# Reordering a four-bit feed-forward by pairs of tiles, and a rotary attention with a third score buffer, in an eight-layer kernel

## The chip, the cores and the metric

The kernel is one program on one core of a Trainium2 chip. The metric is the device time of one execution in microseconds (us), and lower is better. Before the change three runs took 2469.4, 2476.17 and 2476.51 us, a median of 2476.17 us.

## The reference

The program computes two hybrid blocks one after the other on `x` of 8 sequences x 512 tokens x 128 channels. Only two kinds of layer matter here. The rest (a state-space scan, a linear attention, a forgetting attention, small normalised feed-forwards) is not touched.

The four-bit feed-forward occurs twice. Its input is normalised over the channels, rounded to a four-bit grid in blocks of 16, multiplied by four-bit weights, gated, and rounded again:

```python
def fp4_quant_dequant(x):                       # blocks of 16 along the last axis
    scale = jnp.maximum(jnp.max(jnp.abs(xb), axis=-1, keepdims=True) / 6.0, 1e-12)
    q = _GRID[jnp.searchsorted(_MID, jnp.abs(xb / scale))] * jnp.sign(xb / scale) * scale
def fp4_linear(x, w):
    return jnp.einsum('bsk,nk->bsn', fp4_quant_dequant(x), fp4_quant_dequant(w))
gate = fp4_linear(x, w_gate); y = fp4_linear(x, w_up)      # 128 -> 352
h = jax.nn.silu(gate) * y
out = fp4_linear(h, w_down)                                # 352 -> 128
```

The rotary attention occurs once, with 16 heads of 8 channels. Queries and keys are rotated, scores are `q k / sqrt(8)` over the 512 tokens of a sequence, then softmax, values, output projection and residual.

## The kernel before, in words

Every layer is one or more stages. A stage owns its buffers and semaphores and ends in a barrier of all engines. Inside a stage each engine has its own instruction list, written out by hand, and the lists meet only through semaphores. Each engine works strictly in the order of its list.

**The first feed-forward stage, `fx`,** quantises the input in four pairs of sequences, each pair one PSUM tile of 128 x 1024 values. TensorE centres the columns. ScalarE squares and sums them (`moments`). VectorE takes block maxima (`maxima`, L736), refines the root (`roots`), makes the scales (`codes`, L756 to L765, of which `above` is L758 and `both` L762) and multiplies them in (`xn`, L765). ScalarE then takes the scaled magnitude (`size`, L715). Rounding is done by adding and subtracting a large number, `mag = max(size, ROUND)`. VectorE computes `tot = max(size, ROUND) + xn` in one instruction (L770). GpSimd computes `mag` (L786), `q = tot - mag` (L790) and `xq = q * above` (L793). TensorE turns `xq` back and ScalarE stores it.

**The second feed-forward stage, `fh`,** walks over 32 tiles j of 128 tokens, four tiles (`NT`) to a sequence m. Per tile:

- TensorE: `gate(j+1)` (L823), `up(j)` (L827), and for the tile three steps older `end` (L835): three transposes of `hq`, and after each fourth tile the down projection (L842), six matmuls of 512 columns.
- ScalarE: `th = tanh(gate/2)` (L860), `size` of the previous tile (L866), and the two copies `ht` of the transposed tile (L872, L873).
- VectorE: `gt = (th + 1) * gate` (L880), the product with `up` (L883), `tot` of the previous tile (L888), the block maxima (L893), `above` (L896), its reciprocal (L898), and `xn` (L900). After every fourth tile it adds the down projection to the residual X (L912, and L914 for the last).
- GpSimd: `mag` (L921), `q` (L925), `hq` (L928).

There are two gate buffers, three up buffers and two transpose buffers in PSUM.

**The attention stage, `rt`,** walks over 8 sequences in a hardware loop, software-pipelined by `pipeline`. One sequence has 16 steps k. A step has two units of scores (L1912), each two matmuls that fill one of two score buffers of two PSUM banks. ScalarE takes the exponential of each unit (L1975, 128 x 1024 values, 256 in all). TensorE multiplies step k-1 by the values (`values`, L1923, eight matmuls with a ones column for the sum), into one of two output buffers. After every fourth step VectorE copies the output to SBUF (`osb`, L1986). TensorE turns it (`turn`, L1931), VectorE divides. Once per sequence follow `turn_back` (L1938), a copy `otc` on VectorE (L1999), `project` (L1943) and the residual (L2004). GpSimd lays out the values of each sequence (`va`, L1900). SyncE loads the query and key stacks half a sequence ahead.

## Time and profile before

| | |
|---|---|
| median of three runs | 2476.17 us |
| the profiled execution, its own time | 2476.36 us |
| its span | 2474.6 us |
| TensorE / VectorE / ScalarE / GpSimd busy | 79% / 67% / 56% / 41% |
| quantising stage `fx`, twice | 429.6 to 475.2 us, and again from about 729 us |
| feed-forward stage `fh`, twice | 476.1 to 621.6 us, and again from about 776 us |
| attention stage `rt`, once | 2158.6 to 2439.4 us |

Busy shares are averages over some thirty stages with different limits, so they say little about these three. In a row of the timeline the first number is the start, the second the length. A length covers the instruction from its start to its last write, and two instructions of one engine without a wait between them overlap by about 0.09 us. The distance between starts is therefore the better measure. A matmul in this number format is two instructions. "[0.64 <-PE ...]" is idle time before the instruction and what ended it.

### The profile page before, as it was taken

What the parts mean: (1) busy time and instruction counts of PE and PEld (TensorE: products, weight loads), DVE (VectorE), ACT (ScalarE), POOL (GpSimd) and SP (SyncE); (2) the same over time, 40 slices, a digit from 0 to 9 for tenths busy, and PEclk for the clock granted to TensorE, in tenths of its full rate; (3) what the DMA queues carried; (4) which work ended last, traced back from release to release, by engine and by line L of the source; (5) the groups of instructions that cost most, each with busy time, mean ns of one, the idle gap of its engine ahead of it and who ended that gap; (6) DMA issues with size and microseconds to landing.
All of it is one profiled execution on the core that took longest, in us unless ns stands there. A gap on an engine that the chain in (4) does not pass through costs nothing. (4 is left out here: it accounts for less than half of the span.)

```text
span 2474.6 us, 37339 instructions
## 1 busy us (share of the span) xinstructions
PE 1943.5 (79%) x11731; PEld 880.3 (36%) x11731; DVE 1648.7 (67%) x2449; ACT 1395.7 (56%) x2254; POOL 1013.6 (41%) x818
## 2 busy tenths in 40 slices
PE   5458885476784674799999999999998867588887
PEld 2123332333463331344444444444444423222222
DVE  5979995687436866778888888888886436611112
ACT  3446661422343323577777777777775533398884
POOL 0256661666016650245455555555545423700001
PEclk9779996688896877899999999999999978799999
DMA  2000000000000001111111111111111100411110
GB/s 87 0 13 0 0 0 0 0 1 1 0 0 0 1 1 50 37 38 58 57 60 56 59 61 60 56 56 56 60 60 57 44 18 26 102 40 50 44 45 34
DMA packets 66132, 85.94 MB, mean 35 GB/s; under 512 B 13345, under 2 KB 37217, under 8 KB 65889
## 3 DMA queue, kind: packets, MB, share of 16 engines
q1 hardware_dynamic: 60944, 81.37, 10.6%
q10 hardware_dynamic: 5040, 2.72, 0.4%
q8 instruction: 79, 1.29, 0.2%
q14 instruction: 69, 0.56, 0.1%
HBM read 72.12 MB, written 11.93 MB: 34 GB/s over the span
## 5 line engine op out<-in xcount | busy, mean ns | idle before, releaser
L1975 ACT ACTIVATE rt_p<-rt_ps_s 128x1024 f32<-128x1024 f32 x256 | 242.7, 1026 | 43.8 <-PE rt_ps_s L1912 43.1
L1618 DVE SCALAR_TENSOR_TENSOR fu_kv<-fu_ps_kv,fa_vec,fu_kv 128x511 f32<-128x511 f32 x366 | 252.6, 739 | 7.3 <-ACT fu_kv L1526 6.4
L1690 POOL TENSOR_TENSOR fu_p<-fu_p 128x768 f32<-128x768 f32 x64 | 116.9, 1826 | 260.3 <-PE fu_ps_n L1376 256.0
L1346 PE MATMUL fu_ps_s<-fu_qn,fu_kn 64*128 64x512 f32 (+3 forms) x1024 | 190.0, 468 | 7.3 <-ACT fu_p L1513 5.6
L601 POOL TENSOR_TENSOR scan_hC<-scan_h,scan_c 128x1024 f32<-128x1024 f32 x64 | 150.8, 2356 | 82.7 <-DVE scan_h L581 82.7
L1376 PE MATMUL fu_ps_n<-fu_p,fu_vt 128*64 128x512 f32 (+3 forms) x1024 | 166.0, 445 | 0.0
L526 PE MATMUL scan_ps_y<-scan_hC,w_ident 128*128 128x512 f32 x256 | 130.3, 632 | 40.9 <-POOL scan_hC L601 24.3
L1701 POOL TENSOR_TENSOR fu_num<-fu_num,fu_sg 128x512 f32<-128x512 f32 x64 | 81.4, 1272 | 172.1 <-DVE fu_sg L1651 172.1
L581 DVE TENSOR_TENSOR_SCAN scan_h<-scan_dA,scan_ps_b 128x1024 f32<-128x1024 f32 x64 | 146.4, 2287 | 2.2
L1923 PE MATMUL rt_ps_o<-rt_p,rt_va 128*32 128x512 f32 x1024 | 138.1, 612 | 4.6 <-POOL rt_va L1900 3.5
L1404 PE MATMUL fu_ps_kv<-w_XN,fa_wp 128*128 128x512 f32 x244 | 125.1, 636 | 18.1 <-DVE fu_cr L1583 15.4
L1346 PEld LDWEIGHTS fu_ps_s<-fu_qn,fu_kn 64*128 64x128 f32 x1024 | 82.6, 185 | 126.4 <-ACT fu_p L1530 52.1
L1912 PE MATMUL rt_ps_s<-ra_stackq,ra_stackk 48*128 48x512 bf16 x512 | 92.7, 390 | 41.4 <-ACT rt_p L1975 22.6
L1591 DVE SCALAR_TENSOR_TENSOR fu_og<-fu_num,fu_ow,fu_ro 128x512 f32<-128x512 f32 x64 | 81.1, 1267 | 58.0 <-POOL fu_num L1701 49.9
L1685 POOL TENSOR_TENSOR fu_kn<-fu_ks,fu_rb 128x512 f32<-128x512 f32 x64 | 99.1, 1549 | 40.6 <-DMA fu_rb<-rms_rows 40.5
L866 ACT ACTIVATE fh_size<-fh_ps_u 128x352 f32<-128x352 f32 x64 | 29.7, 464 | 151.9 <-DVE fh_ps_u L900 151.9
L1526 ACT ACTIVATE fu_kv<-fu_ps_kv,fa_vec 128x512 f32<-128x512 f32 x122 | 82.1, 687 | 51.4 <-PE fu_ps_kv L1404 47.2
L562 ACT ACTIVATE scan_c<-scan_ps_c 128x1024 f32<-128x1024 f32 x64 | 65.5, 1024 | 75.2 <-POOL scan_hC L601 46.4
L823 PE MATMUL fh_ps_g<-w_gate,ffn_xq 128*128 128x352 f32 x128 | 61.9, 573 | 56.8 <-DVE fh_gt L880 53.7
L1595 DVE TENSOR_REDUCE fu_nm<-fu_ps_m 128x2 f32<-128x1024 f32 x64 | 78.0, 1219 | 42.0 <-PE fu_ps_m L1369 42.0
L1900 POOL COPY rt_va<-ra_v 128x128 f32 x32 | 8.1, 296 | 232.8 <-PE rt_ps_o L1923 232.4
L1651 DVE SCALAR_TENSOR_TENSOR fu_sg<-fu_sg,fu_ps_s 128x512 f32<-128x512 f32 x64 | 44.0, 687 | 81.1 <-ACT fu_sg L1502 80.5
(350 smaller groups left out, 5178.6 us busy)
## 6 DMA issues: line engine op xcount, KB each, us to landing
fu_rb<-rms_rows SPq DMA_DIRECT2D x256, 128.0 KB, 2.9
fu_ro<-rms_rows SPq DMA_DIRECT2D x128, 128.0 KB, 2.9
ra_stackq<-rope_parts SPq DMA_DIRECT2D x168, 32.0 KB
ra_stackk<-rope_parts SPq DMA_DIRECT2D x168, 32.0 KB
rope_parts<-rp_q SPq DMA_DIRECT2D x24, 128.0 KB, 2.0
rope_parts<-rp_k SPq DMA_DIRECT2D x24, 128.0 KB, 2.0
rms_rows<-fu_r SPq DMA_DIRECT2D x14, 192.0 KB, 2.1
w_X<-in_xT SPq DMA_DIRECT2D x4, 512.0 KB
```

The costliest lines, as they stand in the source:

```text
L526: i = pe.matmul(yps[:, :], w.ident[:, :], hC[p % (BEHIND + 2)][:, j, :], start=(p == 0 and j == 0), stop=(p == PAIRS - 1 and j == 1))
L581: dve.tensor_tensor_scan(flat[0], flat[1], flat[2], 0.0, ALU.mult, ALU.add).then_inc(s.scan, 1)
L601: pool.tensor_tensor(hC[p % (BEHIND + 2)][:, :, :], hst[p % 2][:, :, :], csb[p % 2][:, :, :], ALU.mult).then_inc(s.hC, 1)
L1346: pe.matmul(sps[:, h, at:at + T - t * P], k[head(h), t * P:(t + 1) * P], q[head(h), t * P:T], start=(at == 0), stop=False)
L1376: m = pe.matmul(nps[head(h), t * P:T], VT[b % VR][:, t, head(h)], p[:, h, :], start=(t == 0), stop=(t == 2))
L1404: pe.matmul(projected(a, j), wp[:, g, 1 + j, :], XN[:, n, :], start=True, stop=True).then_inc(s.kvp, 1)
L1618: dve.scalar_tensor_tensor(acc, projected(a, k)[:, 0:T - j], vec[:, a % GA, at:at + 1], acc, ALU.mult, ALU.add).then_inc(done, 1)
L1685: pool.tensor_tensor(KN[u % 3][:, :], K[u % KR][:, :], RB[:, 1, :], ALU.mult).then_inc(s.kn, 1)
L1690: pool.tensor_tensor(tail, tail, P13[:, :, 0:3 * P], ALU.add).then_inc(s.d1, 1)
L1912: m = pe.matmul(sps[i][:, e, :], stack[1][rows, 2 * q4 + i, t * P:(t + 1) * P], stack[0][rows, 2 * q4 + i, :], start=True, stop=True)
L1923: m = pe.matmul(ops[q4 % 2][32 * j:32 * j + 32, :], va[:, t, 4 * q4 + j, :], pr[k % 2][j // 2][:, j % 2, :], start=(t == 0), stop=(t == NT ...
L1975: act.activation(pr[k % 2][i][:, :, :], sps[i][:, :, :], ACT.Exp, scale=DH_B ** -0.5).then_inc(s.exp, 1)
```

## The change

Three stages change. In `fx` and `fh` the instruction `mag` moves from GpSimd to VectorE, and `tot` becomes a plain addition of `mag` and `xn`. In `fh`:

- ScalarE applies silu itself. The VectorE instruction L880 is gone, and `w.down` is no longer halved in preparation.
- VectorE works on pairs of tiles. `above`, the reciprocal and `mag` each cover two tiles in one instruction.
- TensorE issues gate and up two tiles ahead, and there are four up buffers in place of three but one transpose buffer in place of two. The transposes run four tiles behind, and the down projection of a sequence comes after the first transpose of the tile group behind it.
- ScalarE issues silu two tiles ahead of `size`.

In `rt` the loops are unrolled. There are three score buffers, one output buffer in place of two, and the transposes share a bank with the projection. `values` runs two steps behind the scores, between the two score units of a step. On VectorE the copy `take(n, 0)` comes between `otc` and the residual.

```diff
-                        dve.scalar_tensor_tensor(tot[k % 2][:, :, :], size[k % 2][:, :, :], ROUND, cps[k % RING][:, :, :], ALU.max, ALU.add).then_inc(s.tot, 1)
+                        dve.tensor_scalar(mag[k % 2][:, :, :], size[k % 2][:, :, :], ROUND, None, ALU.max).then_inc(s.mag, 1)
+                        dve.wait_ge(s.mag, k + 1)
+                        dve.tensor_tensor(tot[k % 2][:, :, :], mag[k % 2][:, :, :], cps[k % RING][:, :, :], ALU.add).then_inc(s.tot, 1)
...
+                        pe.wait_ge(s.tot, max(j - 3, 0))
...
+                    def turn(j):
                         pe.wait_ge(s.hq, j + 1)
-                        pe.wait_ge(s.ht, max(2 * (j - 1), 0))
+                        pe.wait_ge(s.ht, 2 * j)
...
+                    for j in range(G + LAG + 1):
+                        if real(j + 2):
+                            gate(j + 2)
+                            up(j + 2)
+                        k = j - LAG
+                        if real(k):
+                            turn(k)
+                        if k >= NT and k % NT == 0:
+                            down(k // NT - 1)
...
+                    def gated(j):
+                        act.wait_ge(s.g, j + 1)
+                        act.wait_ge(s.h, max(j - NT + 1, 0))
+                        act.activation(gt[j % NT][:, :, :].rearrange(flat), gps[j % 2][:, :], ACT.Silu).then_inc(s.gt, 1)
...
                     for j in range(G + LAG):
+                        if real(j + 2):
+                            gated(j + 2)
                         if real(j):
...
+                            act.wait_ge(s.xn, j + 1)
...
+                    for k in range(G // 2 + 1):
+                        both = (2 * k, 2 * k + 1) if k < G // 2 else ()
+                        for j in both:
                             product(j)
-                        if real(j - 1):
-                            total(j - 1)
-                        if real(j):
+                        if k:
+                            sizes(k - 1)
+                            total(2 * k - 2)
+                            total(2 * k - 1)
+                        for j in both:
+                            maxima(j)
+                        if both:
+                            scales(k)
+                        for j in both:
                             scaled(j)
...
-                    pe.wait_ge(s.exp, count(n, U, u - 1))
+                    u = U * n + 2 * k + i
+                    pe.wait_ge(s.exp, max(u - RING + 1, 0))
...
                             scores(n, k, 0)
+                        if n is not None and k >= 2:
+                            values(n, k - 2)
+                        elif last is not None and k < 2:
+                            values(last, STEPS - 2 + k)
+                        if n is not None:
                             scores(n, k, 1)
-                            if k:
-                                values(n, k - 1)
...
+                            if k >= 7 and k % NT == 3:
+                                turn(n, k // NT - 1)
                         if last is not None:
-                            if k == 2:
+                            if k == 3:
                                 turn(last, GROUPS - 1)
-                            elif k == 4:
+                            elif k == 5:
                                 turn_back(last)
-                            elif k == 7:
+                            elif k == 6:
                                 project(last)
...
                     if last is not None:
+                        take(last, GROUPS - 1)
                         norm(last, GROUPS - 1)
                         dve.wait_ge(s.t2, last + 1)
                         dve.wait_ge(s.f, last)
                         dve.tensor_copy(otc[:, :], fps[:, :]).then_inc(s.otc, 1)
                     if n is not None:
-                        norm(n, 0)
+                        take(n, 0)
```

In VectorE's list, `sizes` is `mag` of a pair, `total` is `tot`, `scales` is `above` with its reciprocal, and `scaled` is `xn`. In ScalarE's list, each step is `gated`, then `size`, then the two `ht` copies of the tile four steps older.

## Rows read from the trace of the kernel before

**Rows 1.** Windows view, first `fh` stage: length, busy time by engine (instructions), granted TensorE clock.
```profile
474.00:624.00 150.00, 100.33 (x279) 52.86 (x278) 113.25 (x233) 44.65 (x132) 89.60 (x96) 0.82 0.00 1
```

**Rows 2.** Timeline of one tile of `fh`: start, length, engine, line, tiles.
```profile
547.38 0.51 DVE L880 SCALAR_TENSOR_TENSOR fh_gt<-fh_th,fh_ps_g 128x352 f32<-128x352 f32 x1
547.50 0.46 ACT L866 ACTIVATE fh_size<-fh_ps_u 128x352 f32<-128x352 f32 x1 [2.75 <-DVE fh_ps_u L900]
547.92 0.53 DVE L883 TENSOR_TENSOR fh_ps_u<-fh_gt,fh_ps_u 128x352 f32<-128x352 f32 x1
...
548.28 0.47 ACT L860 ACTIVATE fh_th<-fh_ps_g 128x352 f32<-128x352 f32 x1
...
548.79 0.52 DVE L893 TENSOR_REDUCE fh_amax<-fh_ps_u 128x22 f32<-128x352 f32 x1
549.22 0.93 POOL L925 TENSOR_TENSOR fh_q<-fh_tot,fh_mag 128x352 f32<-128x352 f32 x1
...
549.34 0.84 DVE L896 TENSOR_SCALAR fh_above<-fh_amax 128x22 f32<-128x22 f32 x1
...
550.23 0.79 POOL L928 TENSOR_TENSOR fh_hq<-fh_q,fh_above 128x352 f32<-128x352 f32 x1
...
550.54 0.53 DVE L900 TENSOR_TENSOR fh_ps_u<-fh_ps_u,fh_inv 128x352 f32<-128x352 f32 x1
550.98 0.51 DVE L880 SCALAR_TENSOR_TENSOR fh_gt<-fh_th,fh_ps_g 128x352 f32<-128x352 f32 x1
```

**Rows 3.** Chain of waits in the first `fh` stage: total us, times, longest.
```profile
DVE fh_ps_u L883 <- PE fh_ps_u L827: 17.2, 8, 3.0
```

**Rows 4.** Timeline of `fh`: down projections at both clock levels, and the next gate.
```profile
501.38 2.85 PE L842 MATMUL fh_ps_y<-fh_ht,w_down 128*128 128x512 f32 x6 [2.33 <-ACT fh_ht L873]
...
504.07 0.76 PE L823 MATMUL fh_ps_g<-w_gate,ffn_xq 128*128 128x352 f32 x2
...
615.73 5.10 PE L842 MATMUL fh_ps_y<-fh_ht,w_down 128*128 128x512 f32 x6 [0.64 <-ACT fh_ht L873]
```

**Rows 5.** Timeline, first and last row of the first `fh` stage.
```profile
476.12 1.28 ACT L860 ACT_TABLE_LOAD   x1 [0.93 <-PEq L72]
...
620.87 0.69 DVE L914 TENSOR_TENSOR w_X<-w_X,fh_ps_y 128x512 f32<-128x512 f32 x1 [9.22 <-PE fh_ps_y L842]
```

**Rows 6.** Groups of instructions by form, VectorE, whole kernel: busy us, mean ns.
```profile
L471 DVE TENSOR_SCALAR ssmd_t<-ssm_dx 128x512 f32 x8 | 3.3, 415 | 0.0
L307 DVE TENSOR_SCALAR prep_mag<-prep_mag 128x1120 f32<-128x1120 f32 x1 | 0.7, 745 | 0.0
```

**Rows 7.** Timeline of the first `fx` stage.
```profile
442.34 1.22 DVE L770 SCALAR_TENSOR_TENSOR fx_tot<-fx_size,fx_ps_c 128x1024 f32<-128x1024 f32 x1
...
443.73 0.20 DVE L758 TENSOR_SCALAR fx_above<-fx_normed 128x64 f32<-128x64 f32 x1
443.82 2.34 POOL L790 TENSOR_TENSOR fx_q<-fx_tot,fx_mag 128x1024 f32<-128x1024 f32 x1
...
444.55 1.70 DVE L762 TENSOR_TENSOR fx_both<-fx_inv,fx_rstd 128x64 f32<-128x64 f32 x1
...
470.61 1.93 POOL L793 TENSOR_TENSOR fx_xq<-fx_q,fx_above 128x1024 f32<-128x1024 f32 x1
```

**Rows 8.** Chain of waits in the `rt` stage: total us, times, longest.
```profile
ACT rt_p L1975 <- PE rt_ps_s L1912: 43.1, 55, 12.9
```

**Rows 9.** Timeline of `rt`.
```profile
2281.81 1.06 PE L1923 MATMUL rt_ps_o<-rt_p,rt_va 128*32 128x512 f32 x8
...
2284.64 0.66 PE L1931 MATMUL rt_ps_t<-w_ident,rt_osb 128*128 128x128 f32 x4
...
2285.23 0.61 PE L1912 MATMUL rt_ps_s<-ra_stackq,ra_stackk 48*128 48x512 bf16 x4
...
2285.74 7.59 ACT L1975 ACTIVATE rt_p<-rt_ps_s 128x1024 f32<-128x1024 f32 x8 [0.48 <-PE rt_ps_s L1912]
...
2306.93 0.68 DVE L1986 COPY rt_osb<-rt_ps_o 128x512 f32<-128x512 f32 x1
```

More of the change, by code:

```diff
@@ L825, in up @@
                     def up(j):
-                        pe.wait_ge(s.tot, max(j - 2, 0))
-                        pe.matmul(ups[j % 3][:, :, :].rearrange(flat), tokens(j), w.up[:, :], start=True, stop=True).then_inc(s.u, 1)
-                    def end(j):
-                        m, t = divmod(j, NT)
+                        pe.wait_ge(s.tot, max(j - 3, 0))
+                        pe.matmul(ups[j % 4][:, :, :].rearrange(flat), tokens(j), w.up[:, :], start=True, stop=True).then_inc(s.u, 1)
+                    def turn(j):
@@ L836, in end @@
                         i.then_inc(s.t, 1)
-                        if t == NT - 1:
-                            pe.wait_ge(s.ht, 2 * (j + 1))
-                            pe.wait_ge(s.x, m)
-                            for c in range(KF):
-                                rows = min(P, FF - c * P)
-                                i = pe.matmul(yps[:, :], w.down[0:rows, c, :], HT[m % 2][0:rows, c, :], start=(c == 0), stop=(c == KF - 1))
-                            i.then_inc(s.y, 1)
-                    gate(0)
@@ L846, in _, with down @@
-                    for j in range(G + LAG):
-                        if real(j + 1):
-                            gate(j + 1)
-                        if real(j):
-                            up(j)
-                        if real(j - LAG):
-                            end(j - LAG)
+                    def down(m):
+                        pe.wait_ge(s.ht, 2 * NT * (m + 1))
+                        pe.wait_ge(s.x, m)
+                        for c in range(KF):
+                            rows = min(P, FF - c * P)
+                            i = pe.matmul(yps[:, :], w.down[0:rows, c, :], HT[m % 2][0:rows, c, :], start=(c == 0), stop=(c == KF - 1))
+                        i.then_inc(s.y, 1)
@@ L859, in _ @@
-                            act.wait_ge(s.gt, max(j - NT + 1, 0))
-                            act.activation(th[j % NT][:, :, :].rearrange(flat), gps[j % 2][:, :], ACT.Tanh, scale=0.5).then_inc(s.th, 1)
-                        k = j - 1
-                        if real(k):
-                            act.wait_ge(s.xn, k + 1)
-                            act.wait_ge(s.mag, max(k - 1, 0))
-                            act.wait_ge(s.tot, max(k - 1, 0))
-                            act.activation(size[k % 2][:, :, :], ups[k % 3][:, :, :], ACT.Abs, scale=STEP).then_inc(s.size, 1)
+                            act.wait_ge(s.xn, j + 1)
@@ L867, in _ @@
+                            act.wait_ge(s.mag, max(j // 2 - 1, 0))
+                            act.activation(size[j // 2 % 2][:, j % 2, :, :], ups[j % 4][:, :, :], ACT.Abs, scale=STEP).then_inc(s.size, 1)
                         k = j - LAG
@@ L902, in _, with maxima @@
-                    for j in range(G + 1):
-                        if real(j):
-                            product(j)
-                        if real(j - 1):
-                            total(j - 1)
-                        if real(j):
+                        dve.tensor_tensor(h, gt[j % NT][:, :, :].rearrange(flat), h, ALU.mult).then_inc(s.h, 1)
+                    def maxima(j):
+                        dve.wait_ge(s.h, j + 1)
+                        dve.tensor_reduce(amax[j // 2 % 4][:, j % 2, :], ups[j % 4][:, :, :], AX_X, ALU.max, apply_absolute_value=True).then_inc(s.amax, 1)
@@ new lines, in scales, with scaled @@
+                    def scales(k):
+                        r = k % 4
+                        dve.wait_ge(s.amax, 2 * k + 2)
+                        dve.wait_ge(s.hq, max(2 * k - 6, 0))
+                        dve.tensor_scalar(above[r][:, :, :], amax[r][:, :, :], ABOVE / 6.0, ABOVE * 1e-12, ALU.mult, ALU.max).then_inc(s.above, 1)
+                        dve.wait_ge(s.above, k + 1)
+                        dve.reciprocal(inv[r][:, :, :], above[r][:, :, :]).then_inc(s.inv, 1)
+                    def scaled(j):
+                        dve.wait_ge(s.inv, j // 2 + 1)
+                        dve.tensor_tensor(ups[j % 4][:, :, :], ups[j % 4][:, :, :], widen(inv[j // 2 % 4][:, j % 2, :], FQ), ALU.mult).then_inc(s.xn, 1)
@@ new lines, in sizes @@
+                    def sizes(k):
+                        dve.wait_ge(s.size, 2 * k + 2)
+                        dve.wait_ge(s.q, max(2 * k - 2, 0))
+                        dve.tensor_scalar(mag[k % 2][:, :, :, :], size[k % 2][:, :, :, :], ROUND, None, ALU.max).then_inc(s.mag, 1)
+                    def total(j):
+                        dve.wait_ge(s.mag, j // 2 + 1)
+                        dve.tensor_tensor(tot[j // 2 % 2][:, j % 2, :, :], mag[j // 2 % 2][:, j % 2, :, :], ups[j % 4][:, :, :], ALU.add).then_inc(s.tot, 1)
@@ L1895, in _ @@
                 pool.wait_ge(s.ones, 1)
-                with pool.Fori(0, B) as i:
-                    wait_apart(pool, w, s.pv, STEPS * i)
+                for i in range(B):
+                    pool.wait_ge(s.pv, STEPS * i)
                     for t in range(NT):
```

121 lines of the change are left out of this document (53 added, 68 removed).

## The prediction

> **What bounds the kernel now.** I first read the windows view of the stages that the diff touches, because the page's busy shares are averages over some thirty stages. In the first `fh` stage VectorE is busy 113 of 150 us, ahead of everyone, and the granted TensorE clock is 0.82 [rows 1]. The timeline of one tile says more [rows 2]: from one L880 to the next is 3.60 us, and VectorE has no idle note in it, so between the down projections VectorE alone sets the pace. Two things are to be seen inside. Instructions without a wait between them start about 0.09 us before the one in front has ended. And `above` (L896), a mere 22 columns, takes 0.84 us: it began at 549.34, GpSimd's `q` ran from 549.22 to 550.15, and `above` ended at 550.18. Such a VectorE instruction waits for GpSimd's running one. The waits view gives the second cost [rows 3]: VectorE stood 17.2 us, in 8 waits, for an `up` queued behind a down projection. A down projection takes 2.69 us from its start to the next gate at 2.4 GHz, and 5.10 us at 1.2 GHz [rows 4].
>
> In `rt` ScalarE is nearly always in the exponential: eight in 7.59 us, one each 0.94 us [rows 9]. A sequence has 32, so 30.2 us is its floor. The waits view adds 43.1 us of waiting for scores, of which 12.9 lie before the stage [rows 8]: 30.2 us inside it, 3.8 per sequence, so 34.0 per sequence.
>
> **`fh`, the pair on VectorE.** By start-to-start distances from [rows 2]: L883 and the `tot` behind it take 0.87 us for two, so 0.44 for an independent instruction on 352 columns, and 0.55 where the next one waits for it. Per pair:
>
> - removed: two L880, at 0.54 each
> - products 0.88, totals 0.88 (the second ends with a lead of 0.09), maxima 0.44 + 0.55, `xn` 0.88
> - added: `mag` on 704 columns. [rows 6] give 415 ns at 512 and 745 ns at 1120, a slope of 0.54 ns a column, so 0.52, and 0.55 with its hand-over
> - `above` 0.2 ([rows 7], 64 columns), plus its wait; reciprocal 0.45. The latter is between the 0.36 that lies from `above`'s end to L900 in [rows 2] at 22 columns and the 0.62 between L758's end and L762 in [rows 7] at 64.
>
> That is 4.8 us. Three waits come on top.
>
> 1. ScalarE's order. Let a be the end of `xn(2k-2)`. ScalarE then does `size(2k-2)` and two `ht` copies (0.78 from L866 to L860 in [rows 2]), then `gated(2k+1)`, 0.47, done at a+1.29. The second product wants it at a+0.8, so VectorE stands 0.5 us. `size(2k-1)` ends at a+1.65, `mag` starts at a+1.76.
> 2. `above` again. `total(2k-2)` ends at a+2.83, so GpSimd runs `q` from 2.93 to 3.86 and `hq` from 3.93 to 4.72. `above` is ready at 4.15 and gets in at 4.72, 0.6 late. `mag` itself meets no one: GpSimd's two tiles end at a+6.7, and the next `mag` comes at a+5.87+1.76.
> 3. `xn(2k)` ends at a+5.87. So a pair takes 5.87 us, 2.93 a tile, for 3.60 before.
>
> The page "SBUF — State Buffer" of the Trainium skill, section "Who interferes with whom", states what the 0.84 us suggests: a `tensor_scalar` in its fast mode and GpSimd exclude each other for the whole instruction. It speaks against moving `mag` to VectorE. Were `mag` to meet a `q` each time, the pair would be up to 0.93 us longer; by the order above it does not.
>
> **`fh`, the down projection.** `up(2k+2)` needs `total(2k-2)`, so it starts at a+2.85. Behind it come a transpose (0.45), the down projection, gate and `up(2k+3)`, which the second product of the next pair wants at a+7.2. By column counts from [rows 4], gate or up is 0.62 us at 2.4 GHz and 1.2 at 1.2 GHz. At the high clock `up(2k+3)` is done at about a+7.6, 0.45 late. At the low clock throughout: up 4.2, transpose 4.9, down 10.0, gate 11.2, up 12.6, 5.4 late. I take 1.6: in [rows 3] the mean wait is 2.15, and the longest, 3.0, is not what the low clock throughout would give, so the clock usually rises during the projection. 0.45 and 5.4 are the ends.
>
> **`fh`, the sum.** The stage starts at 476.1 [rows 5]. Two gates and two ups at the low clock, products, maxima, scales: `xn(1)` ends near 484.4, so 8.3 us. Then 15 pairs x 5.87 = 88.1; six residual additions (0.68 less the overlap) 3.5; six down projections in the way x 1.6 = 9.6. Tail: `mag`, two totals to 2.8, four GpSimd instructions to 6.0, transposes and copies to 7.65, a cold down projection 5.1, X 0.7: 13.5. Sum 123.0 us. Before: 476.12 to 621.56, 145.4. The gain is 22.4 a stage, 45 in the two (59 with every projection warm, 0 with every one cold).
>
> **`fx`.** GpSimd runs `mag`, `q` and `xq` of a pair one after the other and looks like the bound. Taking `mag` away leaves the chain through VectorE, and there the exclusion bites. `mag` on VectorE costs 0.70 (1024 columns by the slope). The first total moves little, ending near T = 443.5 (before: 443.56 [rows 7]). Before, `q` had to wait for GpSimd's own `mag`, and `above` slipped in front of it, at 443.73 against 443.82 [rows 7]. Now `q` is ready 0.1 us after the total, `above` only after 0.17, behind `normed`. So `above` waits the 2.34 of `q`, ends at T+2.65, the reciprocal takes 0.62, and `both` then waits for `xq`, 1.93, as it waited in 1.70 us for `q` before [rows 7]. `xn` ends at T+6.1. Maxima, four small instructions, `mag` and total follow, 3.8. Two periods of 9.9 us and a last one of 9.25 put the last total at 472.55 and the last `xq` at 477.0. Before, it ended at 472.54 [rows 7]. That is 4.4 us lost a stage, 9 in the two. If `above` is first, it waits for nothing, the period is 8.1, and the end is 1 us earlier than before. I take the loss, because `q` has 0.07 us of lead.
>
> **`rt`.** TensorE per step, by starts: values 1.0 (1.06 less an overlap), a pair of score units 0.54 [rows 9], 1.54 against 1.88 of ScalarE. A turn adds 0.59 [rows 9]. Let E be the end of exponential 2k-3. Scores start at E+0.07, `values(k-2)` at E+0.4, done at E+1.5. Exponential 2k needs its buffer at E+1.80, a slack of 0.3. After a turn TensorE is 0.25 late, which now fits in the slack, where before each turn cost about 0.5 (0.48 at 2285.74 [rows 9]). The one output buffer fits too: values, 0.07, copy 0.69, hand-over, 1.88 in all, one step. What does not fit is the boundary of sequences. `turn_back` starts at E+1.62 of step 5. Then come `otc`, 0.7 later, and only 0.6 behind it `take(n, 0)`, done 2.04 after `turn_back`, at E+3.66. `values(4)` wanted to start at E+2.23 and must wait for it. ScalarE stands 1.1. `project` (0.9) directly behind costs 0.6 more, `turn(n, 0)` 0.25, and the late `va` about 0.1. So 2.0 to 2.1 are lost per sequence, not 3.8. 1.8 x 8 = 14.4, say 15 us gained, as the loop's branches go too. The ends are 0 and 30.
>
> **Sum.** 45 - 9 + 15 = 51 us off 2476.4 (the profiled execution's own time; its span is 2474.6, and the median of the runs is 2476.2, so nothing to correct): **2425 us**.
>
> **Rivals.**
>
> - *Cold projections.* TensorE's work in `fh` runs at 1.2 GHz whenever a projection comes, and 5.4 replaces 1.6. The `fh` gain is gone: 2470. For it: the 0.82 [rows 1]. Against it: TensorE has the same columns in less time and stands less before a projection, where it stood 2.33 us [rows 4]. The page "TensorE: Matmul & The Clock Gate", part 1, says that activity releases the throttle; by that rule a denser stage keeps the high clock, which is the 59 us end.
> - *Everything fits.* Warm projections (-14), `above` first in `fx` (-11), attention near its floor (-10): about 2390.
> - *Attention gives nothing,* because the 0.3 us of slack is not there: each turn still stalls ScalarE. 2440.
> - *Slower: the tables of ScalarE.* If Silu does not share a table with Abs and Copy, ScalarE loads one between silu and `size` and one back, at 1.28 us each [rows 5]. Tanh, Abs and Copy needed one load a stage. On the path from a to `mag` lie two, 2.57 us a pair, 38 a stage: 2425 + 77 = 2502. It decides as soon as there are two loads per tile. "ScalarE: Activation LUTs" of the Trainium skill, section "Table sets: the hidden batching unit", says that abs and copy are in every set, which speaks against it; no row here shows Silu.
>
> **Chances.** The forecast with its spread (2405 to 2450) has 0.56, everything fits 0.14, attention nothing 0.1, cold projections 0.1, tables 0.05, and 0.05 for a wait I have not seen that costs 50 us or more. A change of 0.3%, 7 us, is what a measurement of this kernel can tell. Faster by more: 0.56 + 0.14 + 0.1 and a little of the cold case, 0.83. Within: 0.09. Slower: 0.08. The range for 8 in 10 runs from 2395 to 2460; it leaves out half of the cold case, the tables, and the last part of the good one.
>
> **What would show it.** In `fh`: starts of `above` 5.9 us apart, its length 0.6 to 0.8 with its end at the end of an `hq`; VectorE idle 0.5 us before the second product, released by ScalarE; a wait for `up` once per sequence, near 1.6; one table load. In `fx`: `above` near 2.4 us long, the last `xq` near 477. In `rt`: stalls at steps 6 to 8 of a sequence and none at the other turns, 32.2 us a sequence. The prediction is wrong if `above` meets `q` and `hq` differently, since each meeting is worth 0.8 to 2.3 us, or if the clock in `fh` stays low.

## The result: 2411.1 us, and the profile after

The changed kernel takes 2411.1 us (median of 4 runs, 2407.4 to 2414.2), the kernel before on the same chip 2474.5 us: ratio 0.9742, 95% interval 0.9726 to 0.9758. The forecast was 2425 us within 2395 to 2460, so the sign was right and the time lies inside the range, 14 us under the forecast. By medians the gain is 63 us for the 51 that the sum gave. The profiled execution took 2409.0 us, its span is 2407.1 us.

The changed stages can be measured from the load of ScalarE's table that opens a stage to the one that opens the next. Of the kernel after, timeline of ScalarE (opening of `fx`, of `fh`, and of the stage behind it):

```profile
430.04 1.28 ACT L698 ACT_TABLE_LOAD   x1 [14.78 <-PEq L72]
...
479.97 1.28 ACT L862 ACT_TABLE_LOAD   x1 [0.92 <-PEq L72]
...
598.41 1.28 ACT L183 ACT_TABLE_LOAD   x1 [4.48 <-PEq L72]
```

The same differences for all kernels of this study, one profiled execution each, in us (`rt` here counts from the load 95 us ahead of the attention stage to the load behind it, so it holds the preparation of queries and keys too, whose code is the same in all; "last" is from there to the end of the span):

| kernel | fx 1 | fx 2 | fh 1 | fh 2 | rt | last | median |
|---|---|---|---|---|---|---|---|
| before | 46.5 | 45.3 | 146.3 | 146.6 | 376.9 | 34.0 | 2474.5 |
| after | 49.9 | 48.2 | 118.4 | 117.1 | 363.7 | 31.2 | 2411.1 |
| e1 fx comparison on GpSimd | 45.9 | 45.3 | 115.0 | 115.9 | 363.7 | 31.1 | 2399.7 |
| e2 take first | 49.9 | 48.2 | 115.0 | 117.0 | 356.5 | 34.9 | 2406.4 |
| e3 down projection late | 49.9 | 48.2 | 111.4 | 109.4 | 363.8 | 31.2 | 2391.1 |
| e4 fh comparison on GpSimd | 49.9 | 48.2 | 110.6 | 109.6 | 363.7 | 31.2 | 2390.8 |
| e5 tanh | 49.9 | 48.2 | 128.6 | 126.8 | 363.3 | 31.1 | 2449.3 |
| e6 e3 and ScalarE in pairs | 49.6 | 48.2 | 105.8 | 106.2 | 363.7 | 31.2 | 2385.7 |
| e7 steps spread | 49.6 | 48.2 | 119.2 | 120.5 | 355.6 | 34.8 | 2405.0 |
| e8 all of e1, e6, e7 | 46.5 | 45.3 | 105.5 | 105.9 | 357.0 | 33.7 | 2375.0 |
| e9 before, silu alone | 46.5 | 45.3 | 142.7 | 140.0 | 376.6 | 31.2 | 2464.3 |
| e10 fx small ones first | 45.4 | 43.2 | 119.4 | 114.9 | 363.5 | 31.1 | 2400.3 |
| e11 tanh, two buffers (one run) | 49.5 | 48.2 | 126.5 | 141.0 | 461.7 | 34.8 | 2549.4 |
| e12 e6, e7 and e10 | 45.4 | 43.3 | 105.0 | 104.7 | 356.8 | 33.6 | 2370.3 |

Before to after: `fh` -27.9 and -29.5, `rt` -13.2, `fx` +3.4 and +2.9, last stage -2.8. In all -67.1 of the spans' -67.5. One caution on reading the table: stages whose code is the same differ by some us (`fh` 1 is 118.4, 115.0 and 119.2 in after, e2 and e7), so a difference under 4 us in one `fh` stage says nothing by itself.

**`fh`, after.** Windows view (length, busy time and instructions of PE, PEld, DVE, ACT, POOL, granted clock), answering to [rows 1]:

```profile
480.00:598.00 118.00, 87.53 (x272) 46.64 (x272) 87.10 (x184) 43.91 (x129) 54.17 (x64) 0.88 0.00 1
```

VectorE's busy time fell from 113 to 87 us, GpSimd's from 90 to 54, and the clock rose from 0.82 to 0.88. The timeline of VectorE shows a pair:

```profile
520.13 0.59 DVE L897 TENSOR_SCALAR fh_above<-fh_amax 128x44 f32<-128x44 f32 x1
...
522.09 0.52 DVE L887 TENSOR_TENSOR fh_ps_u<-fh_gt,fh_ps_u 128x352 f32<-128x352 f32 x1
523.92 0.53 DVE L887 TENSOR_TENSOR fh_ps_u<-fh_gt,fh_ps_u 128x352 f32<-128x352 f32 x1 [1.31 <-PE fh_ps_u L825]
524.36 0.52 DVE L908 TENSOR_SCALAR fh_mag<-fh_size 128x704 f32<-128x704 f32 x1
...
526.76 0.58 DVE L897 TENSOR_SCALAR fh_above<-fh_amax 128x44 f32<-128x44 f32 x1
...
528.71 0.68 DVE L931 TENSOR_TENSOR w_X<-w_X,fh_ps_y 128x512 f32<-128x512 f32 x1
...
532.58 0.58 DVE L897 TENSOR_SCALAR fh_above<-fh_amax 128x44 f32<-128x44 f32 x1
```

From `above` to `above` are 6.63 us with a down projection in the way, and 5.82 in the next pair, where the residual addition L931 stands. One pair is the distance between two of these starts. The 15 distances of this stage are 4.94 and 5.35 at the start, then 5.77 or 5.78 plain, 5.81 or 5.82 with L931, 6.62 or 6.63 (three) and 8.07 to 8.31 (three) behind a projection. The timeline of TensorE tells these two kinds apart:

```profile
519.88 2.74 PE L840 MATMUL fh_ps_y<-fh_ht,w_down 128*128 128x512 f32 x6
...
533.27 3.46 PE L840 MATMUL fh_ps_y<-fh_ht,w_down 128*128 128x512 f32 x6
```

A projection at the high clock throughout takes 2.74 us and makes 6.6 of the pair; those of 3.23 to 3.96 us, between this and the 5.10 of [rows 4], ran partly at the low clock and make 8.1 or more.

**`fx`, after.** Timeline of the first stage, VectorE and GpSimd, answering to [rows 7]:

```profile
444.33 2.34 POOL L788 TENSOR_TENSOR fx_q<-fx_tot,fx_mag 128x1024 f32<-128x1024 f32 x1 [47.38 <-DVE fx_tot L772]
444.42 2.30 DVE L758 TENSOR_SCALAR fx_above<-fx_normed 128x64 f32<-128x64 f32 x1
446.75 1.93 POOL L791 TENSOR_TENSOR fx_xq<-fx_q,fx_above 128x1024 f32<-128x1024 f32 x1
...
447.35 1.42 DVE L762 TENSOR_TENSOR fx_both<-fx_inv,fx_rstd 128x64 f32<-128x64 f32 x1
```

`q` starts 0.09 us ahead of `above`, and `above`, 0.20 us of work before, now takes 2.30 and ends with it. `both` ends with `xq`.

**`rt`, after.** Timeline of ScalarE over one boundary between sequences, answering to [rows 9]:

```profile
2222.50 26.51 ACT L2001 ACTIVATE rt_p<-rt_ps_s 128x1024 f32<-128x1024 f32 x28 [0.29 <-PE rt_ps_o L1946]
2250.20 1.94 ACT L2001 ACTIVATE rt_p<-rt_ps_s 128x1024 f32<-128x1024 f32 x2 [1.19 <-PE rt_ps_o L1946]
2252.91 1.94 ACT L2001 ACTIVATE rt_p<-rt_ps_s 128x1024 f32<-128x1024 f32 x2 [0.77 <-PE rt_ps_o L1946]
2255.14 7.44 ACT L2001 ACTIVATE rt_p<-rt_ps_s 128x1024 f32<-128x1024 f32 x8 [0.29 <-PE rt_ps_o L1946]
```

28 exponentials without a gap, turns among them, and then stalls of 1.19, 0.77 and 0.29 us.

### The profile page after: what moved, and what is told of

It is laid out like the page before. It is cut to its first block and busy times, and to the rows that moved or that the text cites. A ratio compares the mean times of both kernels' runs of the same rounds, so it can differ in the third digit from the quotient of the medians.

```text
span 2407.1 us, 35881 instructions
## 1 busy us (share of the span) xinstructions
PE 1917.6 (80%) x11731; PEld 872.8 (36%) x11731; DVE 1613.6 (67%) x2361; ACT 1396.5 (58%) x2254; POOL 919.5 (38%) x746
## 5 line engine op out<-in xcount | busy, mean ns | idle before, releaser
L2001 ACT ACTIVATE rt_p<-rt_ps_s 128x1024 f32<-128x1024 f32 x256 | 240.3, 1040 | 32.8 <-PE rt_ps_o L1946 17.4
L526 PE MATMUL scan_ps_y<-scan_hC,w_ident 128*128 128x512 f32 x256 | 132.1, 640 | 40.9 <-POOL scan_hC L601 24.3
L1362 PEld LDWEIGHTS fu_ps_s<-fu_qn,fu_kn 64*128 64x128 f32 x1024 | 82.7, 185 | 126.5 <-ACT fu_p L1546 52.1
L941 POOL TENSOR_TENSOR fh_q<-fh_tot,fh_mag 128x352 f32<-128x352 f32 x64 | 59.4, 929 | 110.7 <-DVE fh_tot L912 110.7
L1548 ACT ACTIVATE fu_p<-fu_ps_s 128x512 f32<-128x512 f32 x64 | 38.2, 597 | 95.4 <-PE fu_ps_s L1370 95.4
L1546 ACT ACTIVATE fu_p<-fu_ps_s 128x1024 f32<-128x1024 f32 x64 | 65.5, 1024 | 47.1 <-PE fu_ps_s L1370 45.8
```

Of the source, the lines that this page charges most:

```text
L526: i = pe.matmul(yps[:, :], w.ident[:, :], hC[p % (BEHIND + 2)][:, j, :], start=(p == 0 and j == 0), stop=(p == PAIRS - 1 and j == 1))
L1362: pe.matmul(sps[:, h, at:at + T - t * P], k[head(h), t * P:(t + 1) * P], q[head(h), t * P:T], start=(at == 0), stop=False)
L2001: act.activation(pr[k % 2][i][:, :, :], sps[(U * n + u) % RING][:, :, :], ACT.Exp, scale=DH_B ** -0.5).then_inc(s.exp, 1)
```

## The experiments

All but e9 start from the changed kernel. Each ratio is to the kernel before on the same chip, with its 95% interval. The kernels ran on different chips, where the kernel before took 2473.3 to 2474.5 us, so medians of two of them compare to about 1 us plus their own spread. The diffs are shortened to the calls that moved.

### e1, `fx`: the comparison back on GpSimd

```diff
-dve.tensor_scalar(mag, size, ROUND, None, ALU.max)      # then wait
-dve.tensor_tensor(tot, mag, cps, ALU.add)
+dve.scalar_tensor_tensor(tot, size, ROUND, cps, ALU.max, ALU.add)
+pool.tensor_scalar(mag, size, ROUND, None, ALU.max)     # ahead of q
```

> This kernel is the changed one with one part undone: in the fx stages the constant comparison (fx_mag) goes back to GpSimd and VectorE makes tot in one operation, as before. Theory (in the changed kernel fx_above waits 2.30 us a pair because GpSimd's q, started 0.09 us earlier, holds both engines' shared access to SBUF, and fx_both waits 1.42 us for fx_xq): the two fx stages come back from 49.93 and 48.18 us to about 46.5 and 45.3, the kernel is 6 us faster than the changed one, 2405 us. Rival (VectorE alone now has enough to do, and the 3.4 and 2.9 us have another source in the stage, such as the clock): no difference in the stage lengths beyond 1 us, 2411 us.

2399.7 us, ratio 0.9714 (0.9682 to 0.9745). The stages are 45.9 and 45.3 us: the 6.9 us of the two stages are back, as the theory has it. The profiled execution is 14.5 us shorter than that of the changed kernel and the median 11; of the former, 4.7 lie in `fh` and 3.3 ahead of the first `fx` stage, where nothing was changed. Only the 6.9 can be put down to the edit.

### e10, `fx`: comparison on VectorE, small operations ahead of it

```diff
     scaled(k)              # xn, before the last line of codes(k)
     maxima(k + 1); roots(k + 1)
+    codes(k + 1)           # normed, above, inv, both
     total(k)               # mag, tot
```

> Changed kernel with one move in the fx stages: the comparison stays on VectorE, but fx_normed, fx_above, the reciprocal and fx_both of the next pair stand ahead of fx_mag and fx_tot instead of behind them, so that VectorE asks for nothing of the kind while GpSimd runs q and xq. Theory (the loss of the move lies in two meetings with GpSimd, 2.30 and 1.42 us a pair, three times a stage): the stages shorten from 49.9 and 48.2 us to 45 or below, at or under those of the kernel before, 6 to 14 us in all: 2397 to 2405 us. Rival (the comparison's own 0.69 us on VectorE's path is the loss, the meetings are slack): less than 1.5 us a stage gained, 2408 to 2411 us. Second rival (fx_tot now comes 1.5 us later behind the four small ones, and GpSimd's q and xq with it): stages of 48 us or more.

2400.3 us, 0.9706 (0.9692 to 0.9721), stages of 45.4 and 43.2. VectorE and GpSimd, second pair:

```profile
448.76 0.20 DVE L758 TENSOR_SCALAR fx_above<-fx_normed 128x64 f32<-128x64 f32 x1
...
449.57 0.23 DVE L762 TENSOR_TENSOR fx_both<-fx_inv,fx_rstd 128x64 f32<-128x64 f32 x1
...
451.74 2.34 POOL L792 TENSOR_TENSOR fx_q<-fx_tot,fx_mag 128x1024 f32<-128x1024 f32 x1 [3.50 <-DVE fx_tot L774]
```

`above` is 0.20 again and `both` 0.23, with the comparison still on VectorE. So it was not the comparison's 0.69 us that cost `fx` its 3 us, but the two meetings with GpSimd: with them gone the stages are 1.1 and 2.1 us under those of the kernel before. One meeting is left in the first pair, where `fx_v` (L748) takes 1.78 us in place of 0.17 as it comes 0.19 us behind `xq`.

### e2 and e7, `rt`: take first, then also the steps spread

```diff
     take(last, GROUPS - 1); norm(last, GROUPS - 1)
+    take(n, 0)
     dve.tensor_copy(otc, fps)
-    take(n, 0)
# e7 also, TensorE: turn(last) at step 2 for 3, turn_back at 4 for 5, turn(n, 0) at 8 for 7
```

> Changed kernel with one move on VectorE: in the rotary attention take(n, 0) stands ahead of the copy otc and its wait. Theory (ScalarE's exps stall at each boundary between sequences because rt_ps_o is taken late: 1.19 + 0.77 + 0.29 us at three of them): the first of these goes, the last ones shrink, 1.0 to 1.5 us a sequence, seven boundaries, 7 to 10 us faster than the changed kernel: 2403 us. Rival (the turns and the projection on TensorE at steps 3, 5, 6, 7 hold the queue whatever VectorE does): the sum of the stalls stays at 2.2 us a sequence and the time at 2411 us; then the spread order of TensorE is what has to change.

> Changed kernel with take(n, 0) ahead of otc on VectorE, and the steps of TensorE between two sequences spread: turn of the last group at step 2, turn back at 4, projection at 6, first turn of the next sequence at 8 instead of 7. Theory (three score buffers hide two steps' lateness, and the stall comes where three steps with extra TensorE work stand next to each other): the stalls of 2.2 us a sequence at the boundary go to 0.3 or less, 30.3 us of exps a sequence instead of 32.5, 15 us faster than the changed kernel, 2396 us. Rival (the stalls move to the new places because each extra step, 0.7 to 1.1 us at TensorE beside a pair of values waiting for ScalarE, costs the same wherever it stands): no more than the gain of the early take, 2402 to 2411 us.

e2: 2406.4 us, 0.9732 (0.9702 to 0.9762); `rt` is 7.2 us shorter. One boundary of it on ScalarE, then one of e7 in a fence of its own:

```profile
2216.04 1.94 ACT L2001 ACTIVATE rt_p<-rt_ps_s 128x1024 f32<-128x1024 f32 x2 [0.75 <-PE rt_ps_o L1946]
2218.27 28.48 ACT L2001 ACTIVATE rt_p<-rt_ps_s 128x1024 f32<-128x1024 f32 x30 [0.29 <-PE rt_ps_o L1946]
```

```profile
2241.47 7.62 ACT L2003 ACTIVATE rt_p<-rt_ps_s 128x1024 f32<-128x1024 f32 x8 [0.30 <-PE rt_ps_o L1946]
2249.85 10.52 ACT L2003 ACTIVATE rt_p<-rt_ps_s 128x1024 f32<-128x1024 f32 x11 [0.77 <-PE rt_ps_o L1946]
```

The 1.19 is gone in both, as the theory of e2 has it. In e7 the other two stalls stand four steps apart, 0.30 and 0.77, for 0.75 and 0.29 next to each other. TensorE's timeline in e7 tells what they are:

```profile
2238.04 1.06 PE L1946 MATMUL rt_ps_o<-rt_p,rt_va 128*32 128x512 f32 x8 [0.27 <-POOL rt_va L1923]
...
2239.36 0.66 PE L1956 MATMUL rt_ps_f<-w_ident,rt_osb 128*128 128x128 f32 x4
...
2247.28 1.12 PE L1968 MATMUL rt_ps_f<-rt_otc,w_outT 128*128 128x512 f32 x2
```

The 0.77 follows the projection (L1968), at step 6 as before, and is no smaller with free steps on both sides. The 0.29 behind the first turn of the next sequence is gone at step 8. In its place stand 0.30 behind the last turn of the old sequence (L1956), which now shares its step with `values` that waited 0.27 us for `va`. So the sum of the stalls is the same and the theory of e7 is wrong; its rival has the sum right, though the projection itself was never moved. e7 took 2405.0 us (0.972, 0.9704 to 0.9736), the same as e2. Of e2's 7.2 us only 4.7 reached the median, and its runs (2402 to 2412) overlap those of the changed kernel (2407 to 2414): the stage is shown to be shorter, the whole kernel hardly. In e2's profile the last stage, whose code is untouched, gave 3.7 back. Windows view of that stage, after and then e2:

```profile
2376.00:2407.00 31.00, 19.83 (x66) 6.21 (x66) 10.56 (x15) 12.95 (x21) 10.45 (x8) 0.92 0.17 68
```

```profile
2368.00:2402.00 34.00, 24.25 (x66) 8.12 (x66) 10.57 (x15) 12.98 (x21) 10.46 (x8) 0.80 0.15 62
```

TensorE does the same 66 instructions in 24.3 us at a granted clock of 0.80, for 19.8 us at 0.92.

### e3 and e6, `fh`: the down projection one step later, then ScalarE in pairs too

```diff
         gate(j + 2); up(j + 2)
         k = j - LAG
+        if k > NT and k % NT == 1: down(k // NT - 1)
         turn(k)
-        if k >= NT and k % NT == 0: down(k // NT - 1)
# e6 also, ScalarE: gated, gated, size, size, four copies for two tiles
```

> Changed kernel with one move on TensorE: in the fh stages the down projection of tile group m stands one step later, behind up(j+2) and ahead of the turn, so that up is not queued behind it. Theory (VectorE's product waits for up, 24.5 us in seven waits over both a stage's start and six down projections, 2.1 us for each of the six, of which about 0.5 is waited for anyway): a stage is 6 x 1.6 = 10 us shorter, the kernel 19 us: 2392 us. Rival one (the turn then is what comes late, and ScalarE's copies and the next down with it; or the projection, at the low clock longer than the gap of 4.2 us, delays the next gate): the wait moves from up to gate and half or less is gained, 2400 to 2408 us. Rival two (the wait is VectorE's own slack): within 0.3% of 2411 us.

> As the kernel with the down projection one step later, and ScalarE too in the order of pairs: silu of both tiles, magnitudes of both, copies of both turns, instead of tile by tile. Theory (VectorE waits about 0.5 us at each second product without a residual add in between, because the silu stands behind the magnitude of the tile before on ScalarE): 0.5 us for each of 8 pairs a stage more than that kernel, up to 7 us in all beyond it. Rival (the copies come later by it and the down projection, or the magnitudes come later by 0.6 us and the sums on VectorE wait for them): 0 or some us slower than the kernel with the late projection alone.

e3: 2391.1 us, 0.9662 (0.9637 to 0.9686). Waits of VectorE in its first `fh` stage, after and then e3 (us in total, times, longest):

```profile
DVE fh_ps_u L887 <- PE fh_ps_u L825: 24.5, 7, 11.9
```

```profile
DVE fh_ps_u L887 <- PE fh_ps_u L825: 12.6, 2, 12.0
DVE w_X L934 <- PE fh_ps_y L840: 12.6, 2, 7.0
...
DVE fh_ps_u L887 <- ACT fh_gt L862: 3.7, 8, 0.5
```

The six waits for a projection, 12.6 us, are down to 0.6; the 12.0 is the start of the stage. What is left in a pair is the 0.5 us behind silu that ScalarE's order was said to cost. The stages gave 7.0 and 7.7 us, not 10: behind the first two all pairs are now 5.77 to 5.83, so 9.9 us went from them, but the two waits before L934 are 12.6 us for 10.4 in the changed kernel, as the last two projections took 5.01 and 4.28 us for 4.26 and 2.84 there and so ran at the low clock for longer. e6 takes the 0.5 too: its plain pairs are 5.22 us, nearly no wait is left on VectorE between first product and tail, 2385.7 us (0.9637, 0.9621 to 0.9653), 9 us less than e3 in the two stages, 5 in the median (the intervals of e3 and e6 overlap). Its pairs with a residual addition are 5.82 us.

### e4, `fh`: the comparison back on GpSimd, tile by tile

```diff
-dve.tensor_scalar(mag, size, ROUND, None, ALU.max)      # once a pair
-dve.tensor_tensor(tot, mag, ups, ALU.add)
+dve.scalar_tensor_tensor(tot, size, ROUND, ups, ALU.max, ALU.add)
+pool.tensor_scalar(mag, size, ROUND, None, ALU.max)     # each tile
```

> Changed kernel with one part undone: in the fh stages the constant comparison goes back to GpSimd, one tile at a time, VectorE makes tot in one operation with the comparison inside, the pairs and silu stay. Theory (VectorE is the bound of a pair at 5.8 us with 4.8 us of work; it would lose 0.52 us of work a pair, but GpSimd gets two more operations a pair, each of about 0.75 us or more, on top of two subtractions and two products): GpSimd at 6 us or more a pair becomes the bound and the shared SBUF access costs VectorE waits; a stage 2 to 12 us longer, the kernel 4 to 25 us slower, 2415 to 2436 us. Rival (the move of the comparison was of no use, all of the gain comes from silu and the pairs): a stage 0 to 8 us shorter, 2395 to 2411 us.

2390.8 us, 0.9667 (0.9642 to 0.9692): the rival is right, the stages are 7.8 and 7.5 us shorter. Windows of its first `fh` stage, then its GpSimd from one pair to the next:

```profile
476.10:586.70 110.60, 83.82 (x272) 44.19 (x272) 75.91 (x168) 43.82 (x129) 88.57 (x96) 0.91 0.00 1
```

```profile
511.02 1.08 POOL L937 TENSOR_SCALAR fh_mag<-fh_size 128x352 f32<-128x352 f32 x1
512.18 0.93 POOL L941 TENSOR_TENSOR fh_q<-fh_tot,fh_mag 128x352 f32<-128x352 f32 x1
513.19 0.79 POOL L944 TENSOR_TENSOR fh_hq<-fh_q,fh_above 128x352 f32<-128x352 f32 x1
...
516.87 1.09 POOL L937 TENSOR_SCALAR fh_mag<-fh_size 128x352 f32<-128x352 f32 x1
```

Here GpSimd is the bound, as the theory said, at 5.85 us a pair without a gap. But that is no more than the 5.8 that VectorE's pair takes in the changed kernel, and VectorE, with 11 us less work, now absorbs the projections in its slack instead of passing them on. In the changed kernel they come on top of 5.8. The edit moves the comparison and also takes it tile by tile again, so that `tot` no longer waits for the second `size`; the two were not separated. And the loss holds for this order of TensorE and ScalarE alone: in e6 the comparison is on VectorE, a plain pair is 5.22 us, less than the 5.85 that GpSimd needs here, and the stages are 105.8 and 106.2 us for 110.6 and 109.6. By these numbers e6 with the comparison on GpSimd would be slower than e6; it was not run.

### e5, e9, e11: what silu is worth

```diff
# e5 and e11, ScalarE then VectorE
-act.activation(gt, gps, ACT.Silu)
+act.activation(th, gps, ACT.Tanh, scale=0.5)
+dve.scalar_tensor_tensor(gt, th, 1.0, gps, ALU.add, ALU.mult)
# e9: the reverse of this in the kernel before.   e11 also: RING = 2 in rt
```

> Changed kernel with silu undone: ScalarE makes tanh of half the gate, VectorE multiplies (tanh + 1) by the gate from PSUM in one operation more a tile, as the kernel before did; pairs, comparison on VectorE and attention stay. Theory (VectorE sets the pair, and this operation took 1.08 us of it in two tiles, or 0.54 each, which is 32 tiles in two stages): 16 us a stage, 35 us in all: 2445 us, so most of the 57 us that the fh stages gained is silu. Rival (the pair is held by the waits for GpSimd and TensorE, and the operation fills them): 10 us or less in all, under 2421 us.

> The kernel before with one part of the change alone: silu on ScalarE in place of tanh, and the operation on VectorE that made the gate of it is gone; one tile at a time, comparison on GpSimd, attention as before. Theory (VectorE alone sets the tile at 3.60 us, 0.54 of it that operation, and what is saved isn't given back): 32 tiles x 0.54 = 17 us a stage, fh stages of 129 us instead of 146, 2440 us in all; the pairs then are worth the rest, some 18 us a stage with the comparison on GpSimd and 11 with it on VectorE. Rival (fh_above, 0.84 us in every tile because it waits for GpSimd, takes the gap as its own, as GpSimd needs 2.9 us a tile): the tile stays above 3.3 us and the stages above 136 us, above 2455 us in all.

> A look at two stages in one kernel, read by the length of each stage, not by the total. In fh: tanh and VectorE's operation for the gate, as in the run that undid silu alone, whose profiled execution (fh stages of 128.6 and 126.8 us, total 2427) was 22 us faster than its four other executions. Theory: these had TensorE at its lower clock for more of the fh stages, so this look, if it is like them, shows stages of about 138 us; rival: the 22 us lie in another stage. In rt: the changed kernel's order with two score buffers instead of three. Theory (the third buffer is what lets a turn pass without a stall): 0.5 us or more lost at each of 32 turns, rt 16 us or more longer than 364, so at least 380. Rival (the order, values two steps back between the two scores of a step, is what gains): rt stays within 3 us of 364.

**e9** is the surprise: 2464.3 us, 0.9963 (0.9946 to 0.998), stages 3.6 and 6.5 us shorter where 17 were expected. The rival gave the right size of the stage with the wrong cause. Windows and waits of its first `fh` stage:

```profile
477.00:620.00 143.00, 100.92 (x273) 50.72 (x274) 88.35 (x200) 42.79 (x130) 89.06 (x96) 0.79 0.00 1
```

```profile
DVE fh_ps_u L881 <- PE fh_ps_u L827: 51.0, 8, 15.9
ACT fh_ht L872 <- PE fh_ps_t L835: 36.4, 8, 5.1
POOL fh_q L923 <- PE fh_ps_t L835: 25.5, 7, 4.1
```

Timeline around two projections:

```profile
530.26 5.49 PE L842 MATMUL fh_ps_y<-fh_ht,w_down 128*128 128x512 f32 x6 [3.04 <-ACT fh_ht L873]
...
537.13 0.53 DVE L881 TENSOR_TENSOR fh_ps_u<-fh_gt,fh_ps_u 128x352 f32<-128x352 f32 x1 [5.27 <-PE fh_ps_u L827]
...
543.67 0.55 PE L835 MATMUL fh_ps_t<-w_ident,fh_hq 128*128 128x128 f32 x3 [0.81 <-POOL fh_hq L926]
...
546.31 0.46 ACT L866 ACTIVATE fh_size<-fh_ps_u 128x352 f32<-128x352 f32 x1 [1.34 <-DVE fh_ps_u L898]
546.67 0.38 ACT L872 ACTIVATE fh_ht<-fh_ps_t 128x256 f32<-128x256 f32 x1
```

VectorE works 25 us less than before (88.4 for 113.3), and `above` is shorter too, 0.42 in the mean. It spends the time waiting for `up`: beside the 15.9 of the start, 35.1 us in seven waits, 5.0 each, where [rows 3] have 17.2 in eight. A plain tile is down from 3.60 to 2.59 us, so the rival is wrong on the tile; the tile with a projection is up from 6.37 to 7.8, and four tiles take 17.0 us where the kernel before mostly has 17.4. Two things stand ahead of `up` in TensorE's queue. The projection now runs at the low clock from end to end, 5.49 us in most sequences, where the kernel before has 2.85 to 4.83. And TensorE stands 3.04 us ahead of it, 2.34 at most before: the last transposes are done at 544.2, but ScalarE copies them at 546.67 only, behind a `size` that waits for VectorE's `xn`. GpSimd has as much to do as before and holds up the transposes too, 0.81 us in this row, but it works 89 of 143 us and itself waits 25.5 us for TensorE, so it does not set the pace. What the clock alone is worth can be read in the second stage, where one projection took 2.85 us and its tile 5.03, for 7.7 to 7.8 with 5.49. What keeps the clock low in e9 was not tried.

**e5** measures the same operation from the other side: 2449.3 us (0.9901, 0.9886 to 0.9916), 38 us more than the changed kernel. Its profiled execution, at a mean clock of 0.918, took 2427 with stages only 10 us longer, while its four others, at 0.907 to 0.908, took 2446 to 2451. So the theory's total is met, but not its 16 us a stage: a plain pair grew from 5.78 to 6.33 us and not by 1.08, which fits a pair of 5.22 us without the wait behind silu (e6) and the 1.08 on top. **e11** shows both cases in one trace, first and second `fh` stage by the windows view:

```profile
478.00:604.00 126.00, 85.40 (x272) 44.88 (x272) 102.61 (x215) 44.65 (x130) 54.29 (x64) 0.91 0.00 1
760.00:901.00 141.00, 101.36 (x276) 52.28 (x275) 102.62 (x215) 45.26 (x131) 54.29 (x64) 0.78 0.00 1
```

VectorE's busy time is the same to 0.01 us, the stage is 14.5 us longer, and TensorE's clock is 0.78 for 0.91. Two such stages would be 29 us, which covers the 22 between e5's executions; that they lie there was not seen in a trace of one of those four, so it stays a likely reading.

In `rt`, two buffers under the new order are ruinous: 461.7 us, 98 more than with three. The ScalarE timeline has a stall in every step, not at the turns alone:

```profile
2289.80 1.94 ACT L2003 ACTIVATE rt_p<-rt_ps_s 128x1024 f32<-128x1024 f32 x2 [0.65 <-PE rt_ps_o L1948]
2292.39 1.94 ACT L2003 ACTIVATE rt_p<-rt_ps_s 128x1024 f32<-128x1024 f32 x2 [0.65 <-PE rt_ps_o L1948]
```

A step is 2.59 us for 1.88: the second scores of a step wait for the exponential that frees their buffer, the values stand behind them, and the next scores behind the values, when ScalarE has run out of work. The order works only with the third buffer.

### e8 and e12, all that gained

> All that is expected to gain, in one kernel: fx comparison back on GpSimd (-6), take early and the steps spread (-15), down projection late (-19), ScalarE in pairs (-7 at most). The parts lie in different stages, so theory says that they add: 2411 - 47 = 2364 us, or 2371 without the pairs' share. Rival (the parts take from one another through the clock, as TensorE falls to its lower clock where it has less to do between waits): above 2380 us.

> The kernel of all that gained (late down projection, ScalarE in pairs, early take, spread steps), but in the fx stages with the comparison on VectorE and the small operations of the next pair ahead of it, instead of the comparison on GpSimd. Theory: 2375 us less what the new order gains over the one of before in fx, 0 to 6 us: 2369 to 2375. Rival (fx gets no shorter than before): within 2 us of 2375.

e8: 2375.0 us, 0.9592 (0.9578 to 0.9607). The stages add up to about what the parts gave alone (`fx` 6, `fh` 24, `rt` 7). It misses the expected 2364 to 2371, because `rt` gave 7 for the 15 in that sum, `fh` 24 for 26, and the last stage took 2.5. e12: 2370.3 us, 0.9579 (0.9561 to 0.9597), 41 us faster than the changed kernel, with `fx` stages of 45.4 and 43.3. Against e8 its stages in `fx` are 3 us shorter; the intervals of the two kernels overlap.

## Why the prediction was right, point by point

- **`fh`, the pair.** 5.87 us predicted, 5.78 measured. `mag` 0.52 as said; `above` 0.58 to 0.59, ending with a `hq`; e3 and e6 show the 0.5 us behind silu and that 5.22 is left without it.
- **`fh`, the residual additions: the term that was mis-sized.** "Six residual additions (0.68 less the overlap) 3.5" came on top of pairs that held the 0.5 us wait for silu. But the addition stands where VectorE would have waited, and hides it: pairs with it are 5.82, not 6.46. e6, where that wait is gone, shows the full price, 5.82 for 5.22. That is 3.3 of the 5.4 us that the stage was forecast too long (123.0 from the table load to the last X; 117.6 measured). The first two pairs, 4.94 and 5.35, and 0.09 a pair are the rest. The second stage was shorter still, by fewer projections at the low clock.
- **`fh`, the tail: right by two errors.** From the last `xn` to the last X, 13.5 us were predicted and 14.2 measured (the head of the stage took 7.5 for 8.3). The last projection was put at the low clock, 5.1 us, and took 2.84. But it started 3.0 us later than said, as its transposes stood behind the projection before it and then passed the single transpose buffer one by one, 1.2 us apart, where the sum had 1.65 us for transposes and copies together:

```profile
586.27 4.26 PE L840 MATMUL fh_ps_y<-fh_ht,w_down 128*128 128x512 f32 x6
590.37 0.49 PE L832 MATMUL fh_ps_t<-w_ident,fh_hq 128*128 128x128 f32 x3
591.59 0.52 PE L832 MATMUL fh_ps_t<-w_ident,fh_hq 128*128 128x128 f32 x3 [0.72 <-ACT fh_ht L879]
...
593.98 2.84 PE L840 MATMUL fh_ps_y<-fh_ht,w_down 128*128 128x512 f32 x6 [0.64 <-ACT fh_ht L879]
```

- **`fh`, the down projection.** 1.6 each predicted. Over a plain pair they cost 0.85 three times and 2.3 to 2.5 three times: 9.9 us, 1.6 in the mean. In the second stage it is four and two, 8.2 us. The two sizes go with the length of the projection, so the mean was right and no single one has it; as the share of long ones changes from stage to stage, that the mean came out is in part luck. The rival of cold projections was wrong for this kernel and its clock 0.88, but it is not a fancy: e9 has it at 0.79 and 0.81, e11's second stage at 0.78.
- **What the sum did not see in `fh`.** It priced the change as one; e4 and e9 take it apart, and the parts are far from additive. Silu alone gives 5 us a stage. With the new structure, and the comparison left on GpSimd, it is 36. The comparison's move then costs 7.6. The prediction priced `mag` on VectorE, 0.55 us a pair, as part of the new pair, but beyond a meeting with GpSimd it did not ask whether the pair would be better without it. In this kernel it is the larger of the two losses, 15 us for 7 in `fx`; by the numbers under e4 it would not be one with the order of e6.
- **`fx`.** Loss by the meeting of `above` and `q`: 4.4 a stage predicted, 3.4 and 2.9 measured. `above` waited as said; the distance between two xn was 9.44 us (439.36 to 448.80), not 9.9. By the page "SBUF — State Buffer" of the Trainium skill, section "Who interferes with whom", issue order decides who blocks. The rows agree: 0.09 us ahead of `q`, `above` took 0.20 [rows 7]; 0.09 us behind it, 2.30; in e10, with no GpSimd instruction running, 0.20. In `fh` the same rule speaks against `mag` on VectorE, and no `mag` there met a GpSimd instruction, 0.52 in the mean of 16. The loss that e4 shows has another cause.
- **`rt`.** Stalls of 1.1, 0.6, 0.25 and 0.1 predicted; 1.19, 0.77 and 0.29 measured, none at the other turns and none of its own for the late `va` (the 0.1); 15 us predicted, 13.2 gained. e2 shows the first to be `take(n, 0)` behind `otc`.
- **Tables of ScalarE.** One load opens each `fh` stage and there is none inside: Silu, Abs and Copy alternated without a load.
- **The rest.** 2.8 us came in the last stage, whose code the change does not touch, at a clock of 0.92, where the kernel before has 34.0 us at 0.86. e2 loses as much there. What sets the clock at its start was not tried.

## What to carry to other kernels

An operation taken from the busiest engine is worth its length only if the waits that it hid are gone too: look for the shared queue before counting instructions (here TensorE's, with `up` behind a projection, and that behind copies on ScalarE), and for the clock at which it works, and move the late step in that queue first. When work can go to either of two engines, compare what is left as slack on the one that takes the irregular delays, not only the busy times, and ask again once the delays are gone: e4 beats the changed kernel, and e6 beats e4. And where two engines can block each other, print who asks first: an order change of a few small instructions was worth 4.7 us a stage at no cost.

## What the runs showed of the hardware

- A 128x64 `TENSOR_SCALAR` of 0.20 us took 2.30 us when it began 0.09 us after a 128x1024 `TENSOR_TENSOR` on GpSimd, and a 128x64 `TENSOR_TENSOR` took 1.42. The `RECIPROCAL` between them was not held up, 0.55 us in either order.
- Undoing silu costs 8 to 10 us a stage at a granted clock of 0.88 to 0.92 (e5, and e11's first stage) and 24 at 0.78 (e11's second), VectorE's work being the same: here TensorE's clock decides the price of an edit on VectorE, through the one wait that they share.
- The comparison costs VectorE 0.52 us for two tiles (128x704) and GpSimd 1.08 us for one (128x352).
